# A graph layer on one core: h turned by VectorE and ScalarE instead of TensorE, the weights set four units behind the own products

## What is computed

```python
h = jnp.maximum(_layernorm(x, axis=-1), 0.0)
deg = jnp.sum(adj, axis=1, keepdims=True) + 1e-05
h_neigh = (adj / deg) @ h
out = h_neigh @ W_neigh.T + b_neigh + h @ W_self.T + b_self
result = x + jax.nn.relu(out)
```

## Time and profile before

| | us |
|---|---|
| median of 3 runs (lowest, highest) | 419.63 (419.06, 420.13) |
| the profiled execution | 419.79 |
| its span | 418.0 |
| TensorE matmul busy | 410.0 |
| VectorE busy | 373.5 |
| ScalarE busy | 207.5 |
| GpSimd busy | 131.2 |

### The profile page before, as it was taken

One profiled execution on the slowest core, in us unless ns is written; L12 is line 12 of the kernel. 1 busy time (PEld: TensorE's weight loads), 2 busy tenths in 40 slices (PEclk: granted clock), 3 DMA queues, 4 the chain that ended last, 5 costly groups with the idle time before them and its releaser, 6 DMA issues.

```text
span 418.0 us, 5575 instructions
## 1 busy us (share of the span) xinstructions
PE 410.0 (98%) x2005; PEld 344.6 (82%) x2005; DVE 373.5 (89%) x461; ACT 207.5 (50%) x266; POOL 131.2 (31%) x107
## 2 busy tenths in 40 slices
PE   7999999999999999999999999999999999999995
PEld 4788888888888888888888988888888888888884
DVE  4899989999999979999599999989797996979944
ACT  3787667745435534553356445345353644526411
POOL 4667477410025912042207214305200302003021
PEclk9999999999999999999999999999999999999998
DMA  8988999899887176546343755535645454454001
GB/s 268 407 285 315 335 289 318 258 247 284 261 274 166 44 283 225 196 153 218 134 150 107 266 181 200 189 121 178 222 151 201 152 201 159 151 194 169 34 0 52
DMA packets 25339, 83.99 MB, mean 201 GB/s; under 512 B 2784, under 2 KB 4320, under 8 KB 25312
## 3 DMA queue, kind: packets, MB, share of 16 engines
q1 hardware_dynamic: 22864, 75.77, 51.2%
q0 software_dynamic: 2016, 7.34, 8.8%
q10 hardware_dynamic: 432, 0.52, 0.4%
HBM read 79.43 MB, written 4.19 MB: 200 GB/s over the span
## 4 chain that ended last, share of the span: by engine, by line
PE 95%; DVE 2%; issue 1%; POOL 1%; DMA 1%; DVEq 0%; POOLq 0%
PE banks L628 76%; PE banks L687 10%; PE banks L678 2%; PE banks L644 2%; PE banks L645 2%; PE banks L646 2%; DMA x_sb<-x_in 1%; DVE adj_lo L437 1%; POOL rstd L273 1%; PE banks L729 0%; PE banks L660 0%; PE banks L661 0%; PE banks L662 0%; DVE own L589 0%; DVE stats L406 0%
## 5 line engine op out<-in xcount | busy, mean ns | idle before, releaser
L304 ACT ACTIVATE adj_hi<-adj_raw 128x1024 fp32r<-128x1024 f32 x127 | 134.0, 1057 | 129.7 <-PE banks L628 127.6
L437 DVE TENSOR_TENSOR adj_lo<-adj_raw,adj_hi 128x1024 fp32r<-128x1024 f32 x127 | 165.4, 1305 | 13.4 <-ACT adj_hi L304 12.9
L449 DVE TENSOR_TENSOR total<-total,adj_raw 128x1024 f32<-128x1024 f32 x106 | 132.8, 1253 | 0.0
L628 PE MATMUL banks<-adj_hi,h_hi 128*128 128x512 f32 x472 | 128.2, 393 | 0.9 <-ACT adj_hi L304 0.9
L628 PE MATMUL banks<-adj_hi,h_lo 128*128 128x512 f32 x472 | 126.4, 389 | 0.3 <-DVE h_lo L429 0.3
L628 PE MATMUL banks<-adj_lo,h_hi 128*128 128x512 f32 x472 | 126.2, 389 | 0.0
L628 PEld LDWEIGHTS banks<-adj_hi,h_lo 128*128 128x128 f32 x472 | 88.5, 188 | 19.4 <-DVE h_lo L429 0.7
L628 PEld LDWEIGHTS banks<-adj_lo,h_hi 128*128 128x128 f32 x472 | 88.6, 188 | 18.5
L628 PEld LDWEIGHTS banks<-adj_hi,h_hi 128*128 128x128 f32 x472 | 86.5, 188 | 18.7 <-ACT adj_hi L304 2.1
L264 POOL TENSOR_TENSOR x_sb<-x_sb,own 128x1024 f32<-128x1024 f32 x7 | 49.2, 7030 | 121.4 <-ACT own L366 121.4
L258 POOL TENSOR_TENSOR own<-own,b_sum 128x1024 f32<-128x1024 f32 x8 | 23.3, 2909 | 80.4 <-ACT own L351 80.4
(11 more groups left out here) (78 smaller groups left out, 337.4 us busy)
## 6 DMA issues: line engine op xcount, KB each, us to landing
adj_raw<-adj_in SPq DMA_DIRECT2D x128, 512.0 KB, 4.2
total_dma<-adj_in POOLq DMA_DIRECT2D x14, 512.0 KB, 8.0
x_sb<-x_in SPq DMA_DIRECT2D x14, 256.0 KB, 7.3
rows_out<-x_sb SPq DMA_DIRECT2D x7, 512.0 KB, 2.9
rows_out<-x_sb SPq DMA_DIRECT2D x3, 128.0 KB, 1.8
x_sb<-x_in ACTq DMA_DIRECT2D x1, 256.0 KB, 6.8
own<-w_neigh SPq DMA_DIRECT2D x1, 256.0 KB, 5.7
own<-w_self SPq DMA_DIRECT2D x1, 256.0 KB, 5.6
```

The source lines that it names most:

```text
L304: nc.scalar.activation(adj_hi[:, s % RING, :, :], adj_raw[:, s % RAW, :, :], ACT.Copy).then_inc(s_hi, 1)
L437: nc.vector.tensor_tensor(adj_lo[:, r, :, :], adj_raw[:, s % RAW, :, :], adj_hi[:, r, :, :].bitcast(F32), ALU.subtract).then_inc(s_lo, 1)
L449: nc.vector.tensor_tensor(total[:, q % 2, :, :], total[:, q % 2, :, :], adj_raw[:, s % RAW, :, :], ALU.add).then_inc(s_add, 1)
L628: done = nc.tensor.matmul(banks[:, MAIN[q % 2][k], :], m[:, j, k * P:(k + 1) * P], part[:, r, a, :], start=(j == 0 and stage == 0), stop=F ...
```

## The change

- **h is turned without TensorE.** turn, turned_high, turned_low and make_h_again go, and with them the identity and two PSUM banks. Instead VectorE transposes the block's h_hi and h_lo in squares of 32 x 32 (turn_squares, 2 + 2 instructions of 128x512), and ScalarE moves the squares to their partitions in ht (move_squares, 16 instructions of 32 partitions x 512 elements, two per unit, three for block 1). The squares lie in buffers that are free then: h_row, own and total_dma now share one tensor, shared.
- **Tables.** own_at and weigh_at are new; the weights stand four units behind the own product (before two, for blocks 5 and 6 seven), products of blocks 1 to 4 are taken two units behind the weights of the block before. take_own stands three units behind the own product.
- **The end.** VectorE finishes three of the last four tiles, GpSimd with ScalarE one; the order of the stores is 0, 1, 3 on SyncE.
- by_dma and the additions by VectorE are as before: all of blocks 2 to 7.

```diff
-    turn_at = [32, 45, 58, 68, 78] + [16 * q + 8 for q in range(5, Q)]
-    own_at = [36, 49, 62, 72, 82] + [16 * q + 11 for q in range(5, Q)]
-    weigh_at = [38, 54, 64, 74, 84] + [16 * (q + 1) + 2 for q in range(5, Q)]
+    own_at = [40, 56, 68, 79, 89, 98, 108, 123]
+    weigh_at = [44, 60, 72, 83, 93, 102, 114, 130]
+    square_at = [30, 48] + [o - 10 for o in own_at[2:]]
+    moves = [2, 3] + [2] * (Q - 2)
     degrees_at = [w + 1 for w in weigh_at[:-1]]
-    product_at = [31, 42, 57] + [last_unit[q] + 3 for q in range(3, Q)]
+    product_at = [31, 46, 62, 74, 85] + [last_unit[q] + 3 for q in range(5, Q)]
     fold_at = [30, 33] + [last_unit[q] + 1 for q in range(2, Q - 1)]
-    halves_at = [(32, 35), (48, 49)]
-    flip_at = [37, 50, 55, 65] + [last_unit[q] + 2 for q in range(4, Q - 1)]
-    runs_at = [38, 51, 58, 68] + [last_unit[q] + 3 for q in range(4, Q - 1)]
+    halves_at = [(32, 35), (47, 48)]
+    flip_at = [37, 51, 55, 66] + [last_unit[q] + 2 for q in range(4, Q - 1)]
+    runs_at = [38, 52, 65, 77, 88] + [last_unit[q] + 4 for q in range(5, Q - 1)]
...
-            def make_h_again(q, t):
-                if q == 0:
-                    act.wait_ge(s_hlo, T // 2)
-                else:
-                    act.wait_ge(s_turned, 2 * q)
-                normalise(q * UI + t, h_row[:, t // 2, 0, :])
-                normalise(q * UI + t + 1, h_row[:, t // 2, 1, :]).then_inc(s_again, 1)
-
-            def turned_high(q):
+            def move_squares(q, n):
+                act.wait_ge(s_square, 4 * q + 4)
                 if q >= 1:
                     act.wait_ge(s_own, 2 * q)
-                for k in range(KC):
-                    act.wait_ge(s_turned, 2 * q + k + 1)
-                    nc.scalar.activation(ht_hi[:, k, :], banks[:, TURNED[k], :], ACT.Copy).then_inc(s_hthi, 1)
+                low = 1 if q == 0 else 3
+                rows = slice(32 * (n // 4), 32 * (n // 4) + 32)
+                feats = slice(32 * (n % 4), 32 * (n % 4) + 32)
+                nc.scalar.activation(ht[feats, :, :, :, rows].rearrange("p l t k r -> p l (t k) r"),
+                                     shared[rows, 0:low + 1:low, :].rearrange("p l (n f) -> p l n f", f=P)[:, :, :, feats],
+                                     ACT.Copy).then_inc(s_ht, 1)
...
-                    if s == own_at[q] + 4:
+                    for n in range(16):
+                        if s == square_at[q] + 2 + n // moves[q]:
+                            move_squares(q, n)
+                    if s == min(own_at[q] + 3, S - 1):
                         take_own(q)
...
+            def turn_squares(q, part):
+                if part == 0:
+                    if q == 0:
+                        dve.wait_ge(s_hhi, PAIRS)
+                        dve.wait_ge(s_hlo, PAIRS)
+                    else:
+                        dve.wait_ge(s_ht, 16 * q)
+                elif q == 0:
+                    dve.wait_ge(s_wlo, 1)
+                elif q == 1:
+                    dve.wait_ge(s_both, 4)
+                source = (h_hi, h_lo)[part]
+                place = 0 if part == 0 else 1 if q == 0 else 3
+                for n in range(2):
+                    tiles = slice(q * UI + 2 * n, q * UI + 2 * n + 2)
+                    nc.vector.transpose(shared[:, place, n * 2 * F:(n + 1) * 2 * F],
+                                        source[:, tiles, :].bitcast(F32).rearrange("p t f -> p (t f)")).then_inc(s_square, 1)
...
-            for t in range(2, UI):
+            for t in range(1, UI):
                 row = (Q - 1) * UI + t
...
-            def turn(q):
...
-                for k in range(KC):
-                    for t in range(UI):
-                        last = nc.tensor.transpose(banks[:, TURNED[k], t * P:(t + 1) * P],
-                                                   h_row[:, t // 2, t % 2, k * P:(k + 1) * P], ident[:, :])
...
             def own_product(q):
-                pe.wait_ge(s_htlo, 2 * q + 2)
+                pe.wait_ge(s_ht, 16 * q + 16)
```

82 lines of the change are left out of this document (26 added, 56 removed).

## The result

| | before | after |
|---|---|---|
| median of 22 executions (lowest, highest), us | 419.72 (419.06, 420.39) | 418.56 (417.43, 420.43) |
| ratio, 95% interval | 1 | 0.9972 [0.9962, 0.9982] |
| profiled execution, its span | 419.79, 418.0 | 419.37, 417.5 |

The changed kernel is 0.3% faster, 1.2 us, where 0.9% was forecast. Two later series of it gave ratios of 0.9968 [0.9951, 0.9985] and 0.9987 [0.9977, 0.9997].

The account below looks back on a forecast made before the run. TensorE, busy 98% with 95% of the chain, was taken as the bound. Span 418.0 - 7.0 + 2.6 + 0.9 + 0.1 + 0.2 - 0.8 = 414.0, plus 1.8 around it: 415.8 us, 0.9% faster; range 412.2 to 419.2.

Parts of the forecast that it names:

- What bounds the kernel, the transposes: TensorE bounds the kernel; removing its 64 transposes, 0.87 us for each block's eight, saves 7.0 us.
- VectorE's transposes: Four transposes a block on VectorE at 0.63 us, less 1.20 for ht_lo: +1.3 us per block, hidden on the average.
- rival 4: VectorE's transposes of h are dearer than that of the sums; at twice 0.63 us, 420.5; chance with the rest 0.05.
- ScalarE's moves, m = 0.52: Each of 16 moves a block paces 0.52 us, bounds 0.49 and 1.0; a three-move unit costs 2.5, under TensorE's 2.72.
- rival 3: ScalarE's moves become the bound at units 50 to 55 and 90 to 93, slower than before; decides from m about 0.77; chance 0.13.
- Check 2: Units 46 to 53: waiting for block 0's weights makes VectorE and ScalarE late; stall 2.1 us, sum 2.6, bounds 0.5 and 4.5.
- W: End of block 0's weights on TensorE; the split of unit 51 was forecast to end at W + 18.7.
- Check 1: Units 30 to 39: VectorE's split of unit 32 comes 0.35 us ahead of need; loss taken 0, bound 0.5.
- Check 3: Blocks 2 to 6: GpSimd's addition delays unit 79 by 0.9 us, bounds 0 and 1.5; addition of the bias near unit 93, 0.1.
- The end: Block 7's take_own and the bias addition delay unit 127's low part, +0.2 us; last tiles and spaced stores, -0.8.
- O: End of block 7's own product on TensorE, 398.66 us before; the addition of unit 127 was forecast at O + 4.95.
- Rival 2: Late ScalarE delays low parts and further closing units; four more places of about 0.65 us, 418.4 in all; chance 0.10.

Follow-up runs that it names:

- the third version: Changed kernel with places reordered: two moves a unit except block 5, most weights nearer own products, half joins of block 1 in slots 48 and 49; 410.55 us, ratio 0.9788.

## Why the prediction was wrong, step by step

- **What bounds the kernel, the transposes**: right. The units' starts give back 0.89 a block, 7.1 us, for 0.87 and 7.0. With all gaps closed the third version is 9.8 us of span under before, of which 1.9 is an earlier start, and 7.9 are the transposes and the end, for which the forecast had 7.0 and 0.8.
- **VectorE's transposes** (0.63 paced, 0.68 busy): right; rival 4 fell.
- **ScalarE's moves, m = 0.52**: the step that failed first; the checks of units 50 to 98 rest on it. The nearest row was a run of instructions of one shape on all partitions; the loss of overlap where groups change is in no row of before. m is 0.65, and the split beside it paces 1.08 instead of 0.95, which the forecast left out. A slot of three is 3.04, in its formula 0.95 + 3m as if m were 0.70, past the 0.59 at which such a slot is longer than a unit. So rival 3 was right in its mechanism; that the kernel came out slower, its other half, fell, since 0.70 is under the 0.77 from which it decided.
- **Check 2** (2.6, measured 4.0 to 4.2): the chain of relu, moves and split was read rightly, the split of 51 ended at W + 18.9 for 18.7, and the gap was 1.84 for 2.1. What was missing is the units behind it at 3.05, or the clock, which no step considered, and 0.57 at unit 50, where the low part (VectorE, last in the same chain) was late and the forecast looked at the high part only.
- **Check 1** (0, bound 0.5; measured 0 to 1.9): it asked when unit 32 wants its low part, and found 0.35 us to spare. Unit 32 waits at its very start for p_lo, which stands behind the transposes; the wait is in the code, and wasn't listed, nor was unit 31, which closes block 1 and wants its low part at its start. Beside that the margin came from a lead of VectorE that one trace had, 3.14 us. The second trace of before has 2.53, the changed kernel and its variants 0.8 to 3.5. In the profiled execution this was the largest single miss, 1.7 us for 0.
- **Check 3**: unit 79 in its mechanism, GpSimd's addition in VectorE's gap, with 1.5 for 0.9, of which the dearer moves are a part. Units 91 to 98: 1.1 for 0.1; the bias held VectorE 2.2 us as forecast (3.42 for 1.21), but the dearer moves had eaten the 0.7 and 1.0 us that ScalarE was to have to spare.
- **The end**: 0.8 for 0.2 before the degree matmul. The addition of unit 127 started at O + 5.4 (O is 398.15 here) instead of O + 4.95, since the low part ahead of it took 3.33 us beside GpSimd's addition of the bias (the earlier trace rows had one of 3.41); behind it the 3.4 of the earlier trace rows held. The last tiles and stores gave 0.7 for 0.8, though SyncE still issued its three stores within 1.31 us, and not spaced as forecast.
- **Rival 2**, doubled stalls, is the nearest by time (418.4). Its reason, late parts spreading to further units, holds for units 51 to 55 only; the other places have causes of their own. That the time fell so near it, and inside the stated range, is luck: losses 5.5 us above the forecast and an unforeseen start 2.0 us earlier partly cancel.

What stays open: whether the removed identity has a part in the earlier start, why the changed kernel's ratio goes from 0.9968 to 0.9987 between series, why the clock falls behind one gap and not behind the other, and how much of the losses at units 79 and 91 to 98 each of the two causes named there has.

## What to carry to other kernels

Where work goes from the engine that sets the end to one that is 63% busy, the sum of busy times says nothing of it: every wait for a freed buffer needs its own check, at the first moment at which the waiter needs it, against a lead read from more than one trace. Before a change is judged, its order should be repaired: here the change in a mended order gave 2.1% (some of it the earlier start, whose cause is open), and in its first placing 0.3%. A repair that moves a step forward can meet a DMA that was never waited for before.
